# A decoder megakernel on one core: another opening, another step order in two stages, and a new table of fill products

## The reference

```python
scores = einsum('bhir,bhjr->bhij', q_lr, k_lr) * scale          # block 9
scores = where(causal_mask, -inf, scores)
y = einsum('bhij,bhjd->bhid', softmax(scores), v)

bidx = cumsum(patch_lens, axis=1) - 1                            # block 10
boundary_mask = zeros((bsz, seqlen)).at[arange(bsz)[:, None], bidx].set(1)
depool = associative_scan(comb, (a_b, u), axis=1)                # a decayed sum over patches
plug = clip(cumsum(boundary_mask, axis=1) - 1, 0, plen - 1)
x = x + depool[arange(bsz)[:, None], plug] + rmsnorm(layernorm(x)) @ W_in.T + b_in
```

## Time and profile before

| | |
|---|---|
| median of 3 runs | 2230.65 us (2230.61 to 2231.53) |
| the profiled execution's own time | 2239.66 us |
| its span | 2237.7 us |
| mean granted TensorE clock | 0.969 |
| busy: PE, DVE, ACT, POOL | 1976.8, 1477.0, 1095.1, 752.9 us |
| fill products | 328 |

### The profile page before, as it was taken

One profiled execution on the slowest core, in us unless ns is written; L12 is line 12 of the kernel. 1 busy time (PEld: TensorE's weight loads), 2 busy tenths in 40 slices (PEclk: granted clock), 3 DMA queues, 4 the chain that ended last, 5 costly groups with the idle time before them and its releaser, 6 DMA issues.

```text
span 2237.7 us, 35565 instructions
## 1 busy us (share of the span) xinstructions
PE 1976.8 (88%) x12266; PEld 1333.1 (60%) x12266; DVE 1477.0 (66%) x4666; ACT 1095.1 (49%) x2785; POOL 752.9 (34%) x776
## 2 busy tenths in 40 slices
PE   6988888998999999887899999778797898888879
PEld 3555456776565564555556777566564456666646
DVE  7666646555565557787633875898886756777753
ACT  2333333666433332687612565688685224666232
POOL 3222134101222232145433554665543331111353
PEclk9999999999999999999999999989999899999899
DMA  6999801100100002101153455200231000000100
GB/s 252 329 335 346 277 0 69 41 20 1 62 1 1 1 1 92 40 29 59 40 201 108 142 149 162 111 1 1 90 126 38 1 1 18 1 1 2 41 1 38
DMA packets 40305, 180.68 MB, mean 81 GB/s; under 512 B 6816, under 2 KB 24352, under 8 KB 36992
## 3 DMA queue, kind: packets, MB, share of 16 engines
q1 hardware_dynamic: 32496, 157.30, 20.6%
q0 software_dynamic: 7632, 21.11, 2.7%
HBM read 155.19 MB, written 98.89 MB: 114 GB/s over the span
## 4 chain that ended last, share of the span: by engine, by line
PE 60%; DVE 22%; ACT 9%; issue 4%; POOL 3%; DMA 1%; POOLq 0%; DVEq 0%; another core or an unknown queue 0%; SPq 0%; ACTq 0%
PE ps L239 41%; PE ps L795 4%; ACT BIG L879 4%; PE ps L780 3%; PE ps L2102 3%; DVE BIG L839 2%; PE ps L814 2%; ACT BIG L338 2%; PE ps L306 1%; DVE XN L295 1%; PE ps L2114 1%; DVE BIG L338 1%; DVE SML L280 1%; DVE XT L338 1%; DVE BIG L3359 1%
## 5 line engine op out<-in xcount | busy, mean ns | idle before, releaser
L239 PE MATMUL ps<-BIG 128*128 128x256 f16 (+2 forms) x1616 | 335.6, 357 | 28.0 <-DVE BIG L2727 12.8
L879 ACT ACTIVATE BIG<-BIG,SML 128x256 f32<-128x256 f32 (+1 forms) x768 | 313.0, 482 | 25.3 <-DVE SML L839 25.3
L239 PEld LDWEIGHTS ps<-BIG 128*128 128x128 f16 (+1 forms) x1616 | 220.3, 138 | 119.7 <-issue 58.3
L795 PE MATMUL ps<-CST,BIG 128*128 128x128 f32 x1408 | 213.2, 286 | 51.9 <-ACT BIG L879 37.6
L338 ACT ACTIVATE BIG<-ps 128x512 f32<-128x512 f32 (+1 forms) x304 | 160.5, 568 | 166.3 <-PE ps L795 154.6
L687 POOL TENSOR_TENSOR BIG<-BIG 128x512 f16<-128x512 f32 x120 | 142.3, 1187 | 276.6 <-ACT BIG L621 248.4
L795 PEld LDWEIGHTS ps<-CST,BIG 128*128 128x128 f32 x1408 | 158.6, 144 | 121.1 <-issue 69.0
L239 PE MATMUL ps<-XN,BIG 128*128 128x512 f16 x864 | 200.7, 387 | 11.3 <-ACT BIG L598 7.0
L839 DVE CUSTOM_DVE_ANT_0 BIG<-ps,BIG 128x256 f32<-128x256 f32 x512 | 181.0, 419 | 35.0 <-PE ps L780 32.9
L243 POOL TENSOR_SCALAR SML<-SML 128x4 f32<-128x4 f32 (+1 forms) x96 | 26.1, 272 | 470.9 <-DVE SML L283 201.6
L602 ACT ACTIVATE BIG<-ps,SML 128x512 f32<-128x512 f32 x88 | 60.4, 686 | 211.8 <-PE ps L239 211.7
(11 more groups left out here) (420 smaller groups left out, 3892.2 us busy)
## 6 DMA issues: line engine op xcount, KB each, us to landing
slots<-in_zeros SPq DMA_DIRECT2D x28, 2640.0 KB, 65.3
WA<-slots SPq DMA_DIRECT2D x95, 132.0 KB
BIG<-in_l1e SPq DMA_DIRECT2D x2, 4224.0 KB
BIG<-spread SPq DMA_DIRECT2D x16, 512.0 KB, 6.6
BIG<-in_l0e SPq DMA_DIRECT2D x8, 768.0 KB, 8.3
BIG<-in_ctxT SPq DMA_DIRECT2D x8, 512.0 KB, 7.6
BIG<-in_ctxT SPq DMA_DIRECT2D x16, 256.0 KB, 3.2
BIG<-in_ctx SPq DMA_DIRECT2D x16, 256.0 KB, 3.4
```

Source lines behind the costliest of these rows:

```text
L239: m = T.e.matmul(ps, l, r, start=i == 0, stop=i == len(pairs) - 1)
L795: m = T.e.transpose(PS[r][:, o:o + P], c["SM"][n % 2 * 4 + i][:, q, tok(k)], ident)
L879: A.e.activation(s[:, q, 0:kn[q]], s[:, q, 0:kn[q]], ACT.Exp, bias=mx[:, q:q + 1], scale=-1.0, accum_out=c["SUM"][b % 2][:, at_sum:at_sum ...
```

## The change

Four edits.

1. The opening. The constants are put in another order and come in two DMAs: 400 columns (identity, the exponent row and a row of ones, signal `turner`) behind the first group of X, and 1100 columns behind the weights. PE and POOL wait for `turner`, DVE for its group of X alone; ACT starts with a one-element Sigmoid. ACT makes seven of the eight copies to XT and seven of the eight to XC, DVE one of each, POOL none; the copies to XC read PSUM instead of XT and stand ahead of the fence. All fills of the opening stand in one place.
2. Stage 9 gets its own `STEPS` and `by=("AVAA",)`: ACT makes `c0` too, after `x3`, and `o2` comes ahead of `x3`.
3. In `patch_dve` the counts, running sum and clamp of batch k-2 stand at the head of step k, ahead of the squares and one-hot rows of batch k.
4. `WARM` has 65 keys for 40, and 491 fill products for 328.

```diff
-MISC = [("ident", 128), ("ones", 128), ("half0", 128), ..., ("mhalf", 16), ("onesrow", 256), ("dst", 64), ("spill", 8)]
+MISC = [("ident", 128), ("mhalf", 16), ("onesrow", 256), ("ones", 128), ..., ("dst", 64), ("spill", 8)]
...
+STEPS[9] = {
+    "pe": ["s t2' t3' . v2 end . t0 . t1 ."],
+    "dve": ["c3' . c2' m0 m1 m2 m3 . c0 . c1 ."],
+    "act": [". c2' c3' x0 x1 . x2 o2 x3 c0 . c1 ."],
+}
...
-    ("xn", 0, 0): 18, ("xn", 0, 1): 11, ("xn", 0, 2): 11, ("xn", 0, 3): 4, ("xc", 0): 6, ("kn", 0): 10, ("dy", 0): 11,
+    ("xn", 0, 0): 27, ("idle", "start"): 2, ("kn", 0): 16, ("dy", 0): 7, ("ktc", 1): 2, ("ktc", 2): 2, ("ktc", 3): 6,
...
-            c = attend(9, 16, [...], [P, 2 * P], get)
+            c = attend(9, 16, [...], [P, 2 * P], get, by=("AVAA",))
...
                     waits(T, *before)
+                    warm(b, "oh", k - 1)
                     waits(T, ("oh", k - 1))
...
             for k in range(B + 3):
+                if 0 <= k - 2 < B:
+                    b = k - 2
+                    waits(V, ("hits", b))
+                    V.e.tensor_scalar(c["CN"], bank("hits", b)[:, 0:256], 1.0, None, ALU.min).then_inc(*V.sig("cn", b))
+                    V.wait_ge(*V.last())
+                    V.e.tensor_tensor_scan(c["PL"][b % 3], onesrow, c["CN"], -1.0, ALU.mult, ALU.add).then_inc(*V.step())
+                    V.wait_ge(*V.last())
+                    V.e.tensor_scalar(c["PL"][b % 3], c["PL"][b % 3], 0.0, 255.0, ALU.max, ALU.min).then_inc(*V.step())
                 if k < B:
...
-                 XT[:, k, g * GT:(g + 1) * GT].rearrange("p (b c s) -> p b c s", b=2, c=4)).then_inc(
+                 bank("xt_t", 0, g, k).rearrange("p (b c s) -> p b c s", b=2, c=4)).then_inc(
...
         def begin_pe(p0):
-            T.wait_ge(*at("cst"))
+            T.wait_ge(*at("turner"))
             for g in range(NG):
                 norm_turn(ring, p0, g)
+            T.wait_ge(*at("cst"))
             fence(T, "start")
...
             for g in range(NG + 1):
                 if g < NG:
                     norm_stats(p0, g, (f"x{g}",))
                 if g:
-                    finish(started_dve(p0, g - 1))
+                    norm_scale(V, p0, g - 1)
+            norm_copy(V, p0, NG - 1, 1)
+            if p0 == 0:
+                chunks_of(V, S0, NG - 1, 1)
...
         def begin_act(p0):
+            A.wait_ge(*at("half"))
+            A.e.activation(sml[:, 862:863], nhalf, ACT.Sigmoid).then_inc(*A.step())
+            for g in range(NG):
+                for k in range(1 if g == NG - 1 else 2):
+                    norm_copy(A, p0, g, k)
+                for k in range(1 if g == NG - 1 else 2):
+                    if p0 == 0:
+                        chunks_of(A, S0, g, k)
             A.wait_ge(*at("cst"))
-            for g in range(NG):
-                finish(tail_act(p0, g))
             fence(A, "start")
...
-                    e.dma_start(CST[:, :], a["cst"]).then_inc(*SP.sig("cst", by=16))
+                    e.dma_start(CST[:, 0:400], a["cst"][:, 0:400]).then_inc(*SP.sig("turner", by=16))
             weights(phases[0])
+            e.dma_start(CST[:, 400:total(MISC)], a["cst"][:, 400:total(MISC)]).then_inc(*SP.sig("cst", by=16))
```

More of the change, by code:

```diff
@@ L25 @@
 SLOTS, CLEAR = 560, 20
-MISC = [("ident", 128), ("ones", 128), ("half0", 128), ("half1", 128), ("tri", 128), ("iota", 256),
-        ("pcol", 2), ("par", 2), ("causal", 256), ("mhalf", 16), ("onesrow", 256), ("dst", 64), ("spill", 8)]
+MISC = [("ident", 128), ("mhalf", 16), ("onesrow", 256), ("ones", 128), ("half0", 128), ("half1", 128), ("tri", 128), ("iota", 256),
+        ("pcol", 2), ("par", 2), ("causal", 256), ("dst", 64), ("spill", 8)]
 WCOLS = {
@@ L96 @@
 STEPS[4]["pe"] = ["s t2' t3' . v2 end . t0 . t1 ."] * 2 + ["s t2' t3' . v2 end . t0 . ."] + ["s t1' t2' t3' . v2 end . t0 . t1 ."]
-WARM = {
[7 rows of a table removed]
+STEPS[9] = {
[3 rows of a table added]
+}
+WARM = {
+    ("xn", 0, 0): 27, ("idle", "start"): 2, ("kn", 0): 16, ("dy", 0): 7, ("ktc", 1): 2, ("ktc", 2): 2, ("ktc", 3): 6,
+    ("qn", 1): 5, ("idle", 0): 8, ("exp", 1, 0, 0): 5, ("exp", 1, 1, 0): 5, ("exp", 1, 14, 3): 3, ("ob", 1, 6): 3,
+    ("ob", 1, 7): 12, ("x16", ("expert", 2, 2), 0): 6, ("x16", ("expert", 2, 4), 0): 6,
+    ("x16", ("expert", 2, 6), 0): 6, ("xn", 3, 2): 14, ("idle", 2): 10, ("scan", 3): 8, ("xn", 4, 2): 3,
+    ("exp", 4, 0, 0): 11, ("exp", 4, 1, 0): 2, ("exp", 4, 11, 0): 7, ("exp", 4, 16, 1): 2, ("exp", 4, 18, 0): 2,
[3 rows of a table added]
+    ("exp", 7, 1, 0): 2, ("exp", 7, 3, 0): 9, ("exp", 7, 11, 1): 2, ("exp", 7, 15, 0): 7, ("xn", 8, 2): 8,
+    ("idle", 7): 13, ("xn", 9, 1): 3, ("xn", 9, 2): 11, ("ob", 9, 0): 2, ("o", 9, 6): 3, ("ob", 9, 7): 2,
+    ("obT", 9, 7): 3, ("idle", 9): 13, ("res", 2): 20, ("sel", 2): 4, ("idle", 10): 12, ("xn", 11, 3): 7,
+    ("x16", ("dense", 11), 1): 6,
 }
@@ L1016, in shared_9 @@
             get = scratch()
-            c = attend(9, 16, [range(o, o + 8, 2) for o in (0, 1, 8, 9)], [P, 2 * P], get)
+            c = attend(9, 16, [range(o, o + 8, 2) for o in (0, 1, 8, 9)], [P, 2 * P], get, by=("AVAA",))
             c["KB"] = [RING[:, 8192 + 512 * i:8704 + 512 * i].rearrange("p (k s) -> p k s", k=2) for i in range(2)]
@@ L2723, in patch_dve @@
                                                  ALU.add).then_inc(*(V.sig("oh", b) if h else V.step()))
-                if 0 <= k - 2 < B:
-                    b = k - 2
-                    waits(V, ("hits", b))
-                    V.e.tensor_scalar(c["CN"], bank("hits", b)[:, 0:256], 1.0, None, ALU.min).then_inc(*V.sig("cn", b))
-                    V.wait_ge(*V.last())
-                    V.e.tensor_tensor_scan(c["PL"][b % 3], onesrow, c["CN"], -1.0, ALU.mult, ALU.add).then_inc(*V.step())
-                    V.wait_ge(*V.last())
-                    V.e.tensor_scalar(c["PL"][b % 3], c["PL"][b % 3], 0.0, 255.0, ALU.max, ALU.min).then_inc(*V.step())
                 yield
@@ L3887, in l0_attn_act @@
             waits(A, ("w0",))
-            for g in range(NG):
-                if g < 3:
-                    chunks_of(A, c, g, 1)
             first = key_act(c, 0)
@@ L3984, in begin_pe @@
             ring = Banks(marks, range(8))
-            T.wait_ge(*at("cst"))
+            T.wait_ge(*at("turner"))
             for g in range(NG):
                 norm_turn(ring, p0, g)
+            T.wait_ge(*at("cst"))
             fence(T, "start")
-            waits(T, ("xt", p0, 0, 0))
+            waits(T, ("xc", 0, 0))
             warm(0, "idle", "start")
         def begin_dve(p0):
-            V.e.memset(nhalf, 0.5).then_inc(*V.step())
-            V.wait_ge(*at("cst"))
+            V.e.memset(nhalf, 0.5).then_inc(*V.sig("half"))
             for g in range(NG + 1):
@@ L3998, in begin_dve @@
                 if g:
-                    finish(started_dve(p0, g - 1))
-            fence(V, "start")
-        def started_dve(p0, g):
-            norm_scale(V, p0, g)
-            if turn_of[p0]:
-                norm_copy(V, p0, g, 1)
-            if split_of[p0]:
-                norm_lower(p0, g)
-            yield
-        def begin_act(p0):
+                    norm_scale(V, p0, g - 1)
+            norm_copy(V, p0, NG - 1, 1)
+            if p0 == 0:
+                chunks_of(V, S0, NG - 1, 1)
+            V.wait_ge(*at("cst"))
+            fence(V, "start")
+        def begin_act(p0):
+            A.wait_ge(*at("half"))
[6 more added lines that the diff above has]
+                        chunks_of(A, S0, g, k)
             A.wait_ge(*at("cst"))
-            for g in range(NG):
-                finish(tail_act(p0, g))
             fence(A, "start")
         def begin_pool(p0):
-            G.wait_ge(*at("cst"))
+            G.wait_ge(*at("turner"))
             for g in range(NG):
                 norm_root(p0, g)
+            if p0 == 0:
+                G.e.memset(S0["sp"], 0.0).then_inc(*G.sig("zero"))
+            G.wait_ge(*at("cst"))
             fence(G, "start")
```

3 lines of the change are left out of this document (removed), and 9 rows, old and new, of the table WARM.

## The result

The changed kernel takes **2205.49 us** (median of 4 runs, 2204.46 to 2208.63), the kernel before 2230.97 us (4 runs, 2230.61 to 2231.53). The ratio is 0.9888, 95% interval 0.9876 to 0.9901: 25 us, or 1.1%, faster. The forecast was 2190.6 us, 40 us faster.

What follows compares the result with a forecast made beforehand. PE was taken as the bound (busy 1976.8 of 2237.7 us), through its waits and half-speed products. Terms 10 + 14 + 8 + 8 = 40 off the profiled 2239.66 gave 2199.7, less 9.0 over the median 2190.6 us; range 2174 to 2208.

Steps and rivals of the forecast that it cites:

- the likeliest case: Whole kernel: the forecast itself, all four terms arriving, 2190.6 us with its own range 2180 to 2200; chance 0.50.
- The opening, 10: Opening: first key product at about 22.7 us instead of 32.66, everything behind moving with it; 10 us, bounds 8 to 12.
- The patch counts, 14: Stage 8: counts at the step's head shorten PE's three count waits and return clock; 14 us, bounds 7 and 18.
- the third rival: Stage 8: DVE stays the bound, its work unchanged and nearly gapless, so only 7 us come: 2197.6; chance 0.08.
- Stage 9, 8: Stage 9: shorter PE waits behind L1508, L958 and L1478, less ACT's extra copy; net 8 us, bounds -5 and +15.
- the rival in which ScalarE holds PE: Stage 9: `c0` on ACT frees its bank later and PE waits; term 0 to -5, 2198.6 to 2203.6; chance 0.13.
- The fills, 8: Outside the opening: 184 more fills, shorter than PE's waits, bring back full clock; 8 us, bounds 0 and 18.
- the fills cost more than all the rest brings: Rival, mainly stages 4, 6 and 7: fills outlast shortened waits; 2231 to 2245; slower or no change 0.03.
- two of these together, about 2206: Whole kernel: two of the shortfalls in clock, stage 9 and stage 8 at once, about 2206; chance 0.10.
- the fourth term: Outside the opening: the 8 us expected from clock returned by 184 more fills.
- fewer than 15: Changed profile's expected sign: fewer than 15 half-speed windows behind the opening, where the profile before had 24.
- waits for the one-hot rows: Sign of error: a wait of PE for these rows, forecast 1.4 us later but needed 3 to 5 us on.

Runs made afterwards that it cites:

- b_open: The kernel before with the new opening alone: 2237.53 us against 2244.95, ratio 0.9963.
- a_sums: The changed kernel with DVE's gate sums of stage 0 later: 2212.11 us, ratio 0.9855 to the kernel before (unmodified changed kernel in the same set 0.9860).
- b_patch: The kernel before with the patch counts at the head of a step alone: 2233.48 us against 2244.95, ratio 0.9938.
- a_patch: The changed kernel with the patch counts back at their old place: 2215.68 us, ratio 0.9936 to the kernel before.
- b_nine: The kernel before with stage 9's own step order and copies on ScalarE alone: 2237.73 us against 2244.95, ratio 0.9966.
- a_oldfills: The changed kernel with the old table of fills outside the opening: 2204.41 us, ratio 0.9884 to the kernel before.
- a_late: The changed kernel without 54 fills of twelve keys that start only after PE's wait has ended: 2194.27 us, ratio 0.9841 to the kernel before.

## Why the prediction was right in the sign and 15 us off in the size

Faster, and inside the range of 2174 to 2208, but outside the likeliest case's own 2180 to 2200: 25 us came and 40 were forecast. Term by term:

**The opening, 10: right at its place, not carried on.** The first key product moved by 10.9, and the steps ahead of it by what was worked out. Two things then took from it. The sentence that failed is "everything behind it is released by the same fence and moves with it". DVE is in order, and ahead of the key norm (L3438) stand 24 sums (L3370). Before, they were done when POOL's root was (48.3 us), and PE waited 2.45 us for the norm; now PE comes 12.6 us earlier to the last key products and DVE only 9.3 earlier to L3438, which PE awaits for 3.44. The chain that ended last, in the stretch from 28 to 60 us, has 36.8% of its time in L3370. The second is the clock: the half-speed window behind the opening moved from the key products (33.5 to 36.9 us before) to the sixteen products (41.6 to 48.4), 6.8 us long for 3.4. Place by place the lead is 10.9 us at the first key product, 12.6 at the last (no half clock there now), 10.3 at the turns (the sums) and 7.4 behind the sixteen products, which take 9.92 us for 7.10. So 2.3 us went at the wait for the norm and 2.8 by the clock. What arrived is 8.3 us (5.6 to 11) by `b_open`.

Six of the 24 sums take 1.36 to 1.51 us in place of 0.42. They are the ones that run while POOL multiplies the gates (L3422, 1.26 to 1.51 us each, reading from the same memory). The Trainium skill ("SBUF — State Buffer", Who interferes with whom) says that a DVE instruction with two inputs in SBUF contends with a GpSimd instruction that reads SBUF, and calls the ports that they share an exclusive lock. The trace agrees: each of the six ends 0.27 to 0.29 us after the POOL instruction beside it, as the first two sums shown under `a_sums` do behind these (of the changed kernel too):

```profile
25.09 1.27 POOL L3422 TENSOR_TENSOR BIG<-BIG 128x512 f32<-128x512 f32 x1 [7.09 <-ACT BIG L3402]
26.65 1.27 POOL L3422 TENSOR_TENSOR BIG<-BIG 128x512 f32<-128x512 f32 x1 [0.29 <-ACT BIG L3402]
```

It is no part of the loss, though: before, five sums and the first of the four norms met POOL (that norm took 1.48 us for 0.48), now six sums and no norm.

**The patch counts, 14: right.** 14.8 at the place; 13.9 by `b_patch` and 10.7 by `a_patch`, each with an interval of some 3 to 4 us either way. The next thing to be late is what the text named, the one-hot rows. It was wrong that they cost nothing: PE waited for them for 2.8 us in two before, which the prediction did not count, and waits 5.2 in five now, because PE, without its long waits, reaches them sooner. The waits for the count fell by 10.6 us (12.8 to 2.2), about the 10.5 of the sum; in the same stretch those for the one-hot rows rose by 2.8 and one for L2748 (0.5) came in; the other 7.5 of the 14.8 are PE's products at full clock, for 7.8 in the sum. DVE is the bound of the stretch, as the third rival had it, yet at a rate that leaves nearly the whole sum.

**Stage 9, 8: right mechanism, slightly large.** 6.9 at the place, 7.6 by `b_nine`. The wait behind L1508 is gone (3.9, as forecast). That of L927 for its source, L958, fell by 0.5 (3.6 to 3.1) and not by half (1.8). That for ACT's L1478 fell by 2.2 and not by 3.8, and now stands ahead of the turns. The other side was mis-sized too: ACT's extra copy held nobody. PE's waits for ACT's 128x384 copies are 0.7 us together, so the rival in which ScalarE holds PE did not come.

**The fills, 8: failed.** 0 on top of the rest (`a_oldfills`), 6.5 alone on the kernel before, where 7.3 of it came in stage 4 beside the unexplained idle times. The step that failed is "the fills are shorter than the wait; at full clock they cost nothing". I compared lengths and did not ask when a fill may start. It needs its own bank of PSUM free, and for twelve keys that bank comes free with or after the very event that PE awaits. These 54 fills take 19.1 us and cost 10.5 to 11.2 against the changed kernel's first set, 3.4 to 3.8 in the last. The clock did come back, as the term had it: 27 us of half clock went with the table (112.7 to 85.3), and without the late fills it is worth about 10 (`a_late` against `a_oldfills`). The rival "the fills cost more than all the rest brings" had the cost right in kind and its ground wrong: it asked for waits that are gone, while here the waits are there and the fills stand on the wrong side of them. It forecast a slower kernel, which did not come.

**The base.** The forecast was made against a profile 0.4% over its own median, and the difference was carried over as a constant. About 13 us of that profile's stage 4 (231 us for 217 in `a_oldfills`) go with the idle times of DVE, and of the 27.3 us of half clock from 1047 to 1133 half is gone in `a_oldfills`, which has the old fills there but not the idle times: this clock was not the fills' to win. The profiles differ by 35 us and the medians by 25; the 10 us between are mostly this.

Added up, the parts as measured give between 23 us (8.3, 10.7, 4 and 0) and 36 (8.3, 13.9, 7.6 and 6.5), and 25 came. The prediction had a case of "two of these together, about 2206". That the time is 2205.5 is luck as far as that case goes: only the fourth term fell away, the third rival held in kind and cost next to nothing, and the rest is made of pieces of 1 to 4 us that no rival named.

Of what the changed profile was to show, these came true: the key product at 21.8, the count wait under 1.5, full clock at the patch steps, no wait for L1508's counterpart, about 24.3 us a batch (25.2 less the 0.9 that the shift gains each), a clock of 0.98. Not so: 17 windows for "fewer than 15", and waits for the one-hot rows, which were listed as a sign of error.
